# Two decoder layers on one core: k's rotary step on VectorE, q's left on GpSimd

## What is computed

```python
x = x + softmax_attention(layernorm(x))                 # layer 0, 16 heads
x = x + cross_attention(layernorm(x), ctx)              # 16 heads, softmax
x = x + linear(layernorm(x))                            # int4 weights + low rank
# layer 1, attention with sigmoid weights:
q = rms_norm(z, qn) @ q_w.T + q_b ; k = rms_norm(z, kn) @ k_w.T + k_b
q, k = rotary(q), rotary(k)       # x*cos + pair_swapped(x)*sin
w = sigmoid(q k^T / 4);  w = w / (sum(w) + 1e-8)
x = x + (w @ v) @ o_w.T + o_b
x = x + cross_attention(layernorm(x), ctx)              # one head of 256
x = x + 0.5 * (x_chunk @ expert[e1] + x_chunk @ expert[e2])   # hashed choice
```

## Time and profile before

| | |
|---|---|
| median of 3 runs | 1219.28 us (1215.75 to 1221.16) |
| the profiled execution | 1216.0 us, span 1214.2 us |
| mean granted clock of TensorE | 0.96 of full speed |
| busy: TensorE / VectorE | 1095.4 / 795.6 us |
| busy: ScalarE / GpSimd | 639.3 / 586.4 us |
| sigmoid periods with a rotation of k | from about 704 to 962 us of the span |

### The profile page before, as it was taken

One profiled execution on the slowest core, in us unless ns is written; L12 is line 12 of the kernel. 1 busy time (PEld: TensorE's weight loads), 2 busy tenths in 40 slices (PEclk: granted clock), 3 DMA queues, 4 the chain that ended last, 5 costly groups with the idle time before them and its releaser, 6 DMA issues. The chain is left out here.

```text
span 1214.2 us, 24303 instructions
## 1 busy us (share of the span) xinstructions
PE 1095.4 (90%) x8458; PEld 804.5 (66%) x8458; DVE 795.6 (66%) x1753; ACT 639.3 (53%) x1192; POOL 586.4 (48%) x894
## 2 busy tenths in 40 slices
PE   6678999999999999999999899999999995999975
PEld 4345676676666776677666676777767664778853
DVE  4656777777776556666667877778787632466761
ACT  2234565665664665555553456666666672554430
POOL 3522534444333344555566878777777500023343
PEclk9788999999998999999999899999999997999995
DMA  7966466464663344434430666667576831025456
GB/s 198 122 78 112 63 82 98 73 89 59 98 78 53 60 81 81 78 84 85 86 71 10 86 73 83 75 77 82 69 89 74 97 41 36 13 80 168 132 154 190
DMA packets 123626, 104.94 MB, mean 86 GB/s; under 512 B 26841, under 2 KB 123241, under 8 KB 123497
## 3 DMA queue, kind: packets, MB, share of 16 engines
q1 hardware_dynamic: 118882, 100.76, 51.5%
q10 hardware_dynamic: 4624, 2.63, 1.0%
HBM read 29.47 MB, written 4.19 MB: 28 GB/s over the span
## 5 line engine op out<-in xcount | busy, mean ns | idle before, releaser
L606 ACT ACTIVATE l_probs<-l_sT 128x1024 f32<-128x1024 f32 (+1 forms) x320 | 325.4, 1022 | 83.8 <-PE l_o L964 50.4
L810 DVE TENSOR_REDUCE l_nmax<-l_ring 128x2 f32<-128x512 f32 (+1 forms) x384 | 254.9, 677 | 144.4 <-PE l_ring L979 142.6
L948 PE MATMUL l_sT<-qstack,kstack 99*128 99x256 bf16 (+2 forms) x1280 | 193.5, 275 | 12.2 <-ACT l_probs L606 4.5
L979 PE MATMUL l_ring<-kstack,qstack 96*128 96x256 bf16 (+1 forms) x1024 | 151.8, 252 | 26.4 <-DVE x_res L858 16.4
L964 PE MATMUL l_o<-l_probs,v_heads 128*32 128x256 f32 (+1 forms) x2560 | 162.4, 386 | 1.1 <-ACT l_probs L606 0.9
L948 PEld LDWEIGHTS l_sT<-qstack,kstack 99*128 99x128 bf16 (+2 forms) x1280 | 125.1, 105 | 38.7 <-issue 11.5
L979 PEld LDWEIGHTS l_ring<-kstack,qstack 96*128 96x128 bf16 x1024 | 77.6, 99 | 88.7 <-DVE x_res L858 23.1
L1031 PE MATMUL l_ring<-wT,l_zT 128*128 128x256 f32 x512 | 125.4, 387 | 1.8 <-DVE l_nmax L810 1.6
L964 PEld LDWEIGHTS l_o<-l_probs,v_heads 128*32 128x32 f32 (+1 forms) x2560 | 72.2, 110 | 64.5 <-issue 19.6
L1011 PE MATMUL l_copy<-l_zT,wT 128*128 128x256 f32 x384 | 108.1, 410 | 3.8 <-ACT l_q L652 3.1
L1031 PEld LDWEIGHTS l_ring<-wT,l_zT 128*128 128x128 f32 x512 | 92.5, 191 | 20.9 <-issue 8.8
(11 more groups left out here) (193 smaller groups left out, 1892.7 us busy)
## 6 DMA issues: line engine op xcount, KB each, us to landing
qstack<-l_qpart SPq DMA_DIRECT2D x288, 128.0 KB, 4.2
kstack<-l_kpart SPq DMA_DIRECT2D x192, 128.0 KB, 5.8
t_experts<-in_experts SPq DMA_DIRECT2D x60, 256.0 KB, 3.0
kstack<-l_kpart SPq DMA_DIRECT2D x96, 60.0 KB, 3.2
out_y<-x_res SPq DMA_DIRECT2D x16, 256.0 KB, 3.7
x_res<-in_x SPq DMA_DIRECT2D x1, 2048.0 KB, 15.7
l_cx<-in_ctx SPq DMA_DIRECT2D x16, 90.0 KB, 3.0
t_cx<-in_ctx SPq DMA_DIRECT2D x16, 90.0 KB, 3.2
```

What stands on the lines that cost most here:

```text
L606: act.activation(probs[g % 4][0:kp, :], sT[g % 2][0:kp, :], ACT.Sigmoid if sig(u) else ACT.Exp, scale=HD ** -0.5).then_inc(p_ok, 1)
L810: dve.tensor_reduce(nmax[u % 2][:, tt, h0:h0 + hb], bank("s", u, i)[:, 0:hb * sk].rearrange("p (h k) -> p h k", h=hb), AX_X, ALU.max, nega ...
L948: i = pe.matmul(sT[g % 2][0:kp, j * S:(j + 1) * S], kstack[u % SLOTS][0:rows_used, col * width(u) + kt * kp:col * width(u) + (kt + 1) * kp ...
L979: m = pe.matmul(out[:, j * sk:(j + 1) * sk], qstack[u % SLOTS][0:STACK, (h0 + j) * S + tt * P:(h0 + j) * S + (tt + 1) * P], kstack[u % SLO ...
```

## The change

`rotate` becomes a helper that takes the engine, and both engines call it. `rope_q` stays on GpSimd with `tok_sin`. `rope_k` is issued by VectorE, with the first weight matrix's place in `wT` (`in_q`, last read for the self units) as its scratch. The wait for `tok_ok` and the count of `rot_ok` stay.

```diff
--- before.py
+++ after.py
@@ -475,6 +475,15 @@
             p3 = parts[w][u % 2]
             eng.tensor_tensor(p3[2][:, 0:wd], whole[w][:, 0:wd], p3[1][:, 0:wd], ALU.subtract).then_inc(third_ok[w][sig(u)], 1)
 
+        def rotate(eng, w, u, link, tok_sin):
+            pair = lambda a: a.rearrange("p (x two h) -> p x two h", two=2, h=HH)
+            tok_w = tok[w][:, :]
+            eng.tensor_tensor(pair(tok_sin)[:, :, 0], pair(tok_w)[:, :, 1], pair(t["sin"][:, :])[:, :, 0], ALU.mult)
+            link(eng.tensor_tensor(pair(tok_sin)[:, :, 1], pair(tok_w)[:, :, 0], pair(t["sin"][:, :])[:, :, 1], ALU.mult))
+            link(eng.tensor_tensor(tok_w, tok_w, t["cos"][:, :], ALU.mult))
+            eng.tensor_tensor(tok_w, tok_w, tok_sin, ALU.add).then_inc(rot_ok[w], 1)
+            eng.wait_ge(rot_ok[w], u - 2 * B + 1)
+
         @block.gpsimd
         def _(pool):
             own, factors_done = [0], [0]
@@ -525,16 +534,6 @@
                 link(pool.tensor_tensor(nrest[:, :, :], m[:, :, :], nparts[:, :, 0, :], ALU.subtract))
                 link(pool.tensor_copy(nparts[:, :, 1, :], nrest[:, :, :]))
                 pool.tensor_tensor(nparts[:, :, 2, :], nrest[:, :, :], nparts[:, :, 1, :], ALU.subtract).then_inc(n_ok, 1)
-
-            def rotate(w, u):
-                n = u - 2 * B + 1
-                pool.wait_ge(tok_ok[w], n)
-                pair = lambda a: a[:, :].rearrange("p (x two h) -> p x two h", two=2, h=HH)
-                pool.tensor_tensor(pair(tok_sin)[:, :, 0], pair(tok[w])[:, :, 1], pair(t["sin"])[:, :, 0], ALU.mult)
-                link(pool.tensor_tensor(pair(tok_sin)[:, :, 1], pair(tok[w])[:, :, 0], pair(t["sin"])[:, :, 1], ALU.mult))
-                link(pool.tensor_tensor(tok[w][:, :], tok[w][:, :], t["cos"][:, :], ALU.mult))
-                pool.tensor_tensor(tok[w][:, :], tok[w][:, :], tok_sin[:, :], ALU.add).then_inc(rot_ok[w], 1)
-                pool.wait_ge(rot_ok[w], n)
 
             def first_factors(n):
                 pool.wait_ge(x_stats, n + 1)
@@ -592,8 +591,9 @@
                         add_bias(job, u, t["bc_l_o" if sig(u) else "bc_x_o"])
                     elif job == "fxb":
                         add_bias(job, u, t["bc_ffn"])
-                    elif job in ("rope_q", "rope_k"):
-                        rotate(job[-1], u)
+                    elif job == "rope_q":
+                        pool.wait_ge(tok_ok["q"], u - 2 * B + 1)
+                        rotate(pool, "q", u, link, tok_sin[:, :])
 
         @block.scalar
         def _(act):
@@ -901,6 +901,9 @@
                         normalise(u, i)
                     elif job in ("pb", "fb"):
                         residual(job, u)
+                    elif job == "rope_k":
+                        dve.wait_ge(tok_ok["k"], u - 2 * B + 1)
+                        rotate(dve, "k", u, link, t["wT"][:, 0, :, :].rearrange("p k f -> p (k f)"))
                     elif job in ("st", "fst"):
                         stats(u, "fb" if job == "fst" else "pb")
                     elif job in ("p0q", "p0k") and by_vector(job[2], u):
```

## The result

| | before | after |
|---|---|---|
| median us | 1218.63 (1215.75 to 1221.16, 4 runs) | 1247.10 (1244.42 to 1250.32, 4 runs) |
| ratio after to before | | 1.024, 95% interval 1.0217 to 1.0263 |
| profiled execution, span | 1216.0, 1214.2 | 1250.3, 1248.5 |
| mean granted clock of TensorE | 0.960 | 0.949 |

The change makes the kernel 2.4% slower. The medians are 28.5 us apart, the two profiled executions 34.3: single executions of the changed kernel spread over 6 us, and the profiled one is the slowest of its four.

What follows compares the result with a forecast made beforehand. TensorE, busy 90% of the span, bounds the kernel, held up by VectorE in the sigmoid stage. 17.2 us without the clock plus 14.7 for it made 31.9; 1216.0 became 1247.9, plus 3.3 to the median: 1251 us, range 1230 to 1272.

Steps and rivals of the forecast that it cites:

- The loop and its two legs: Sigmoid periods: two paths from VectorE to TensorE's aT transposes, the longer decides; each of ten periods pays in full, 10.8 us.
- ScalarE leg: Path from VectorE's k subtraction through ScalarE's second k part and e3 to aT: 0.79 us slack, +1.08 us a period.
- late periods: Last three sigmoid periods, where aT has no wait for attn and no slack: 1.87 us each, 5.6 us together.
- Rival C: Sigmoid stage: only VectorE's path through attn to aT counts; 4 to 6 us slower, 1225 us; chance 0.05.
- `attn` leg: Path from VectorE's k subtraction and linear-layer rows through attn to aT: no slack, +0.42 us a period.
- The DMAs and q's rotation: DMAs of k's first part, some 2 us later, and q's rotation, unchanged on GpSimd: both cost nothing.
- Insertion and relief: VectorE, sigmoid periods: k's rotation adds 2.46 us; silent GpSimd shortens cast and subtraction by 0.59, rows by 1.45.
- rival D: VectorE runs the rotation fast enough, say at the cast's rate, that relief wins: about 1217 us; chance 0.04.
- The clock: TensorE's pause before e3's last quarter grows to about 2.0 us; 1.7 us clock fall in two periods of three: 14.7 us.
- Rival A: TensorE's longer gaps cause no fall of the clock: 17.2 us slower, 1236.5 us; chance 0.22.
- rival B: A long clock fall of TensorE in each period, 44 us in all: 1280 us; chance 0.12.
- The cross periods: First three rotations: +1.6 us in the first period, -0.8 in the other two; together +0.8.

Runs made afterwards that it cites:

- e3: Changed kernel with ScalarE's e3 (exponentials, here sigmoids, for the last quarter of TensorE's times-values group) ahead of k's second part: 1232.67 us, ratio 1.0129.

## Why the prediction was right, and where its terms were off

It gave 1251 us and a range of 1230 to 1272; the median is 1247.1. The forecast was a loss of 31.9 us; the medians are 28.5 apart. The mechanism held; that the total came so near is in part luck, as the last points show.

- **The loop and its two legs: right.** A period at full clock takes 21.89 us, +1.06 where 1.08 was worked out, because the ScalarE leg with its slack of 0.79 is the longer one. Moving `e3` alone showed the other leg at +0.40 for +0.42. The late periods grew by 1.84 for 1.87. Rival C, the `attn` leg alone, is what the kernel with `e3` moved does, not this one. C's price of 4 to 6 us does not hold even there: that kernel is 16.3 us slower than the one before, for its clock fell too and it has the same cross periods. The DMAs and q's rotation, which the prediction put at nothing, show in no wait of a matmul from 704 to 946.
- **Insertion and relief: right in the sum.** The rotation took 0.68, 0.41, 0.69, 0.69 us. The first half, beside GpSimd's last instruction of q, was 0.27 above the 0.41 of the second: more than the row's 0.19 that I took. The Trainium skill, SBUF — State Buffer, section "Who interferes with whom", would have it wait to the end of GpSimd's instruction. By that GpSimd, which ends at 740.73, would hold the 0.41 until then and let it end at 741.14; it ended at 741.01. The trace lies between the two: 0.13 us short of what the page gives, 0.08 above my row. From the end of `tokk` to the cast's start it is 2.64 us, where it was 0.21, so 2.43 were put in for 2.46 forecast, and the subtraction ends 1.85 us later for 1.87.
- **Not slower (rival D): fell.** Two f32 inputs ran at 0.69 us for 128x512, not at the cast's rate of 0.42.
- **The clock: right in kind, priced too high.** A short fall in two periods of three was forecast, and in the nine periods of equal make six had one. But the term was 14.7 us for 13 periods. In the profile seven of 13 had a fall, and six of them made their periods 1.2 to 1.6 us longer, the seventh 1.7; together 9.8 (17.66 - 9 x 1.06 = 8.1, and 3.53 - 1.84 = 1.7). Each fall took 1.7 us of TensorE's work, of which a part was hidden where TensorE had waited 0.34 us for `attnT`: that wait occurs 7 times now, 10 before. Filling the gap gave about 6 us back in the medians, less than half of the 14.7. Rival A (no fall) has its like in the kernel with the filled gap, but its sum does not: A has 17.2 us more than the kernel before, this kernel 21.7. Its 1237.35 comes near A's 1236.5 only because the kernel before was 3.6 us faster beside it. Falls as long as rival B's came in each period only at a gap of 4.74 us. B was argued down with a slow stretch that "held a good part of waiting"; but TensorE was busy there for 6.39 of 7 us.
- **The cross periods: the step that failed.** "In the other two nothing waits right behind the rotation" is wrong for the one that ends at 724.29: statistics and the residual addition stand behind it, and TensorE's `oT0` waits for the latter, 1.97 us; the bias addition on GpSimd stretched the rotation there as in the first. In the first the wait for the row maxima was 2.13 where 0.37 + 1.6 was forecast, which is near, but the clock fell behind it, and the term had no clock in it. Sum of the three stretches without the +1.06 of the ordinary leg: 2.89 + 0.26 + 3.37 - 1.06 = 5.5 us, where +0.8 was forecast. The two subtractions gave what was forecast: the waits for `attn` went from 2.05 and 1.36 to 1.65 and 0.97 us. Some of the 5.5 is no cross cost: with the first three rotations on GpSimd the last of the stretches (692.76 to 716.72) was still 1.54 longer than before, not 1.06. TensorE waits 2.7 us for `l_probs` in this first sigmoid unit, where the kernel before waited 0.87 and then 0.50 for `attn`.
- **The sum** of the profiled execution: 16.1 for the legs (forecast 16.4), 9.8 for the clock (14.7), 5.5 for the cross periods (0.8), 31.4 in all (31.9). That these agree is luck: two errors of 4.9 and 4.7 us cancel. And the whole difference of the profiled executions is 34.3, not 31.4, because 2.9 lie outside the stretches. In the medians the same terms read: 21.7 us without the falls in the sigmoid periods (forecast 17.2; the stretches give 16.1 + 5.5 = 21.6), 6 to 7 for those falls (14.7), 28.5 in all (31.9). So there the two errors cancel only in part, and the 3.4 us between 31.9 and 28.5 are most of the 3.9 by which the forecast is too high. The 3.3 us added to get from a profiled execution to a median fitted the kernel before alone: the profiled execution of the changed kernel was 3.2 *above* its median.

What stays open is why the clock falls behind some of twelve equal gaps and not behind others, and whether the cross periods cost the median as much as the profile.

## What to carry to other kernels

Before moving work to an engine with idle time, ask what stands behind it in that engine's order until the next wait that TensorE feels: 2.5 us at the wrong place cost 28.5 us over the kernel, and the same four instructions some 6 us later in each sigmoid period (with the first three rotations left on GpSimd) saved 10. Look for the idle stretch that lies between the producer's end and the consumer's start, and move the work there and not where its input becomes ready. And cost a new gap of TensorE twice, once for the wait and once for the slower clock that can follow it.

## What the runs showed of the hardware

- **Work moved off GpSimd made the engine that took it over less busy.** VectorE's total fell by 4.9 us although it took over 64 instructions: two rows instructions went from 2.18 to 0.73 us, a subtraction of 128x512 f32 from 1.09 to 0.69 once GpSimd was silent. Beside GpSimd's instructions with two SBUF inputs the same kinds took up to 1.67 (a tensor_tensor of 128x512 f32, 0.69 alone) and 1.40 (a cast of 0.43) in the kernel with more work on GpSimd. That it would be so much was not expected.
- **The clock is not a fixed function of the gap.** In the changed kernel twelve gaps ended at 745.61 to 992.24, each 1.86 or 1.87 us long. Seven of the first nine were followed by a fall, the other two and the last three by none. Neither was the gap of 2.70 us that ended at 723.72, while with the first three rotations on GpSimd one of 2.71 ended at 715.71 in a fall (715.5 to 719.5). Nine gaps of 1.34 us gave four falls. Four gaps of 1.76 us in the softmax stage gave none (one is in the earlier trace rows, the others end at 188.66, 233.07 and 277.13), and with 0.23 us left of the gap there was none in 259 us. The wait at the second cross aT, 2.05 us before and 2.03 in the kernel with the late rotation, was followed once by 3.4 us lost (in 673 to 680) and once by 1.7 (in 673.5 to 677.5). In the changed kernel it was 1.65 us, and 3.4 us were lost behind it (678.5 to 685.5).
- **What a fall costs.** Every fall listed here took 1.7 us of TensorE's work or 3.4: 1.7 in each of the cases from 746 to 931; at the gap of 4.74 us the clock was 0.46 short over 7.5 us, 3.4 us, of which some lay in the gap itself. A part comes back where TensorE would have waited behind it anyway.
